# 16-bit denominators with queries split on GpSimd, a bias that ScalarE writes, and VectorE's sums of squares moved behind the split of qz

## The reference, cut to what matters

```python
def reference(x, ...):                      # x: 2 x 4096 x 512, float32
    x = x + _layernorm(_L0_attn_ref(_layernorm(x), w_qkv, w_proj, b_proj))
    x = x + _layernorm(_L0_ffn_ref(_layernorm(x), ...))

def _L0_attn_ref(x, w_qkv, w_proj, b_proj): # 16 heads of 32
    q, k, v = jnp.split(x @ w_qkv.T, 3, axis=-1)
    q, k = relu(q), relu(k)
    ksum = k.sum(over the sequence)
    z = 1.0 / (jnp.einsum('bhd,bhdn->bhn', ksum, q) + eps)
    context = jnp.einsum('bhdn,bhen->bhde', v, k)
    out = jnp.einsum('bhde,bhen->bhdn', context, q) * z
    return out @ w_proj.T + b_proj
```

## Time and profile before

| | us |
|---|---|
| median of 3 runs | 2459.85 (2457.72 to 2460.81) |
| the profiled execution | 2460.71 |
| its span, first to last instruction | 2458.9 |

### The profile page before, as it was taken

How to read it: one execution, slowest core, us unless ns; L and a number is a source line. 1 busy time by engine, 2 the same in 40 slices (tenths; PEclk the granted TensorE clock), 3 DMA queues, 4 the chain that set the end, 5 groups by cost and what they waited for, 6 DMA issues and landing times.

```text
span 2458.9 us, 56923 instructions
## 1 busy us (share of the span) xinstructions
PE 2400.0 (98%) x20208; PEld 1433.9 (58%) x20208; DVE 1805.9 (73%) x3548; ACT 1580.2 (64%) x3473; POOL 1136.8 (46%) x929
## 2 busy tenths in 40 slices
PE   5999999998999999999999999999999999999997
PEld 2444444454666666666666666666666666666664
DVE  5444444426888888888888888888888888888885
ACT  3222323226777777777777777777777777777774
POOL 2587533313444444444444444444444444444444
PEclk9999999999999999999999999999999999999999
DMA  5634434311111111111111111111111111111111
GB/s 137 202 99 126 103 103 102 85 56 35 40 47 47 51 43 47 43 43 43 43 44 50 50 45 48 43 43 43 43 43 47 50 48 46 43 43 43 43 29 32
DMA packets 250704, 145.65 MB, mean 59 GB/s; under 512 B 208096, under 2 KB 208096, under 8 KB 250144
## 3 DMA queue, kind: packets, MB, share of 16 engines
q1 hardware_dynamic: 240048, 119.32, 19.6%
q10 hardware_dynamic: 9504, 17.31, 1.9%
q0 software_dynamic: 1104, 8.40, 0.9%
HBM read 61.09 MB, written 33.55 MB: 38 GB/s over the span
## 4 chain that ended last, share of the span: by engine, by line
PE 93%; POOL 3%; DVE 2%; ACT 1%; issue 1%; DMA 1%; POOLq 0%; SPq 0%; DVEq 0%; ACTq 0%
PE psum L319 17%; PE psum L320 16%; PE psum L321 16%; PE psum L592 6%; PE psum L457 5%; PE psum L494 5%; PE psum L447 4%; PE psum L474 4%; PE psum L503 3%; PE psum L514 2%; PE psum L331 2%; PE psum L368 2%; PE psum L367 2%; PE psum L466 2%; PE psum L366 1%; PE psum L429 1%
## 5 line engine op out<-in xcount | busy, mean ns | idle before, releaser
L319 PE MATMUL psum<-wb,region 128*128 128x512 f16 x768 | 293.0, 381 | 0.0
L320 PE MATMUL psum<-wb,region 128*128 128x512 f16 x768 | 291.6, 380 | 0.0
L321 PE MATMUL psum<-wb,region 128*128 128x512 f16 x768 | 291.6, 380 | 0.0
L1077 POOL TENSOR_TENSOR region<-region,kfac 128x512 f32<-128x512 f32 x64 | 66.7, 1042 | 482.9 <-DVE kfac L1335 482.9
L1060 POOL TENSOR_TENSOR region<-region 128x1024 f32<-128x1024 f32 x64 | 147.8, 2309 | 258.7 <-DVE region L1443 230.2
L1443 DVE SCALAR_TENSOR_TENSOR region<-psum,region 128x512 f16<-128x512 f32 x64 | 44.2, 691 | 222.4 <-ACT region L887 222.4
L1065 POOL TENSOR_TENSOR region<-region 128x1024 f32<-128x1024 f32 x64 | 150.5, 2352 | 93.2 <-DVE region L1208 93.2
L1072 POOL TENSOR_SCALAR region<-region,m 128x512 f32<-128x512 f32 x256 | 172.3, 692 | 26.5 <-DVE hm L1279 26.5
L592 PE MATMUL psum<-region 128*128 128x512 f16 x768 | 176.2, 379 | 2.1 <-DVE region L1443 2.1
L1081 POOL TENSOR_TENSOR region<-region 128x512 f32<-128x512 f32 x64 | 81.8, 1277 | 202.7 <-ACT region L795 202.7
L1242 DVE SCALAR_TENSOR_TENSOR region<-psum,m,region 128x512 f32<-128x512 f32 x192 | 144.1, 751 | 6.8
(11 more groups left out here) (236 smaller groups left out, 7208.3 us busy)
## 6 DMA issues: line engine op xcount, KB each, us to landing
region<-x_in SPq DMA_DIRECT2D x128, 256.0 KB, 2.6
q_cols<-region ACTq DMA_DIRECT2D x64, 256.0 KB, 2.5
region<-q_cols SPq DMA_DIRECT2D x64, 256.0 KB, 2.8
out_rows<-region SPq DMA_DIRECT2D x62, 256.0 KB, 2.0
region<-wb_in POOLq DMA_DIRECT2D x1, 3072.0 KB, 13.4
region<-wqkv_in SPq DMA_DIRECT2D x4, 512.0 KB, 6.9
region<-region SPq DMA_TRANSPOSE x128, 3.0
region<-ws_in POOLq DMA_DIRECT2D x1, 1280.0 KB, 7.6
```

What stands on the lines that cost most here:

```text
L319: mm(out, lhs(0), rhs(0), start=start, stop=False)
L320: mm(out, lhs(0), rhs(1), start=False, stop=False)
L321: return mm(out, lhs(1), rhs(0), start=False, stop=stop)
```

## The change

The denominators are made of 16-bit parts: the sums of the keys are scaled, split (`ks16`) and put into two block matrices (`kden`), and GpSimd splits the loaded queries of tile n+3 in step n (`ahead_queries`), between `front_k2` and `front_state`; `den` waits for that (`q16_ok`) and issues 12 products in place of 4. The bias is no product any more: ScalarE copies it to the bank (`ahead_bias`), after it has waited for VectorE's qz, and the products add to it. VectorE's `back_norm` stands behind `ahead_qz_split`. The queries are stored with their scale of 64, and the factors of the totals are changed to suit; GpSimd no longer prepares `bias16`. The transposed copies of ScalarE signal once per path in place of twice.

```diff
--- before.py
+++ after.py
@@ -80,9 +80,9 @@
...
-        bias16 = sb("bias16", C, dt=f16)
...
-        kden = sb("kden", BATCH, KT, P)
+        kden, ks16 = sb("kden", 2, BATCH, KT, P, dt=f16), sb("ks16", 2, BATCH * KT, dt=f16)
+        q16 = sb("q16", 2, 2, KT, P, dt=f16)
...
@@ -321,21 +321,26 @@
...
             def den(n, p, b, at=0, back=True):
-                pe.wait_ge(S(f"qb{p}_in"), loads(n, p))
+                pe.wait_ge(S("q16_ok"), n * 2 + 2)
...
-                    last = mm(bank[at][:, g * P:(g + 1) * P], kden[:, b, g, :], qb[:, p, g, :], start=True, stop=True)
+                    to = bank[at][:, g * P:(g + 1) * P]
+                    mm(to, kden[:, 0, b, g, :], q16[:, p, 0, g, :], start=(g == 0), stop=False, skip_group_check=True)
+                    mm(to, kden[:, 0, b, g, :], q16[:, p, 1, g, :], start=False, stop=False, skip_group_check=True)
+                    last = mm(to, kden[:, 1, b, g, :], q16[:, p, 0, g, :], start=False, stop=True, skip_group_check=True)
...
             def y_mm(n, b, at=0):
...
-                mm(bank[at], ones16[:, :], bias16[:, :], start=True, stop=False)
+                pe.wait_ge(S("bias_ok"), n + 1)
...
-                    last = mm3(bank[at], lambda x: qz16[:, x, g, :], lambda x: mix[b][:, x, g, :], False, g == KT - 1)
+                    mm(bank[at], qz16[:, 0, g, :], mix[b][:, 0, g, :], start=False, stop=False, skip_group_check=True)
+                    mm(bank[at], qz16[:, 0, g, :], mix[b][:, 1, g, :], start=False, stop=False, skip_group_check=True)
+                    last = mm(bank[at], qz16[:, 1, g, :], mix[b][:, 0, g, :], start=False, stop=(g == KT - 1), skip_group_check=True)
...
@@ -448,9 +453,8 @@
...
             def scores(n, path):
-                kT, qT, where, k_ready, q_ready = ((k1T, q1T, (2, 5), "k1T_ok", "q1T_ok"), (k2T, q2T, (4, 6), "k2T_ok", "q2T_ok"))[path]
-                pe.wait_ge(S(q_ready), cur(n))
-                pe.wait_ge(S(k_ready), cur(n))
+                kT, qT, where, ready = ((k1T, q1T, (2, 5), "path1_ok"), (k2T, q2T, (4, 6), "path2_ok"))[path]
+                pe.wait_ge(S(ready), cur(n))
@@ -687,9 +691,9 @@
...
-            def to_cols(n, dst, where, k, done):
+            def to_cols(n, dst, where, k):
...
-                ac(dst.rearrange("p a b -> p (a b)"), bank[where], ACT.Copy).then_inc(S(done), 1)
+                return ac(dst.rearrange("p a b -> p (a b)"), bank[where], ACT.Copy)
...
@@ -726,6 +730,10 @@
...
+            def ahead_bias(n, at=0):
+                act.wait_ge(S("qzf_ok"), n + 1)
+                ac(bank[at], bproj[:, :], ACT.Copy, scale=QZ_SCALE).then_inc(S("bias_ok"), 1)
...
@@ -803,12 +811,12 @@
             def front_transposed(n):
...
-                to_cols(n, q1T, 5, 0, "q1T_ok")
-                to_cols(n, k1T, 2, 1, "k1T_ok")
+                to_cols(n, q1T, 5, 0)
+                to_cols(n, k1T, 2, 1).then_inc(S("path1_ok"), 1)
...
             def front_transposed2(n):
-                to_cols(n, q2T, 4, 2, "q2T_ok")
-                to_cols(n, k2T, 6, 3, "k2T_ok")
+                to_cols(n, q2T, 4, 2)
+                to_cols(n, k2T, 6, 3).then_inc(S("path2_ok"), 1)
...
@@ -852,6 +860,7 @@
...
+                    ahead_bias(n + 2)
@@ -890,8 +899,7 @@
...
-                ac(q4[:, :, m, :], bank[3].rearrange("p (t c) -> p t c", t=GT), ACT.Relu,
-                   scale=1.0 / W_SCALE).then_inc(S("q_read"), 1)
+                ac(q4[:, :, m, :], bank[3].rearrange("p (t c) -> p t c", t=GT), ACT.Relu).then_inc(S("q_read"), 1)
...
@@ -948,7 +956,9 @@
...
+            ahead_bias(0)
...
+            ahead_bias(1, at=5)
@@ -1012,9 +1022,6 @@
             def late_bias():
...
-                then_step(nc.gpsimd.tensor_scalar(bias16[:, :], bproj[:, :], 1.0, 1.0, ALU.mult, ALU.mult))
-                low = slice(HALF, P)
-                then_step(nc.gpsimd.tensor_tensor(bias16[low, :], bproj[low, :], bias16[low, :], ALU.subtract))
...
@@ -1104,12 +1111,23 @@
...
-            def step(n, p, front=True, back=True):
+            def ahead_queries(n, p, again=True):
+                wait_alone(pool, S(f"qb{p}_in"), loads(n, p))
+                if again:
+                    wait_alone(pool, S("den_pe"), n)
+                nc.gpsimd.tensor_scalar(q16[:, p, 0], qb[:, p], 1.0, 1.0, ALU.mult, ALU.mult).then_inc(S("q16_ok"), 1)
+                pool.wait_ge(S("q16_ok"), n * 2 + 1)
+                nc.gpsimd.tensor_tensor(q16[:, p, 1], qb[:, p], q16[:, p, 0], ALU.subtract).then_inc(S("q16_ok"), 1)
...
+            def step(n, p, front=True, back=True, ahead=True):
...
+                if ahead:
+                    ahead_queries(n + 3, 1 - p)
+                if front:
@@ -1137,13 +1155,18 @@
...
+            ahead_queries(0, 0, again=False)
+            ahead_queries(1, 1, again=False)
...
+            ahead_queries(2, 0)
...
-            with pool.Fori(1, ALL - 1, 2) as n:
+            with pool.Fori(1, ALL - 3, 2) as n:
...
-            step(ALL - 1, 1)
-            step(ALL, 0, front=False)
+            step(ALL - 3, 1, ahead=False)
+            step(ALL - 2, 0, ahead=False)
+            step(ALL - 1, 1, ahead=False)
+            step(ALL, 0, front=False, ahead=False)
@@ -1400,9 +1423,6 @@
...
-                if back:
-                    back_norm(m)
-                if front:
@@ -1411,6 +1431,8 @@
...
+                if back:
+                    back_norm(m)
@@ -1464,15 +1486,22 @@
...
+                totals = flat(ksum_c[:, :, :])
+                ve.tensor_scalar(ks16[:, 0], totals, W_SCALE / SEQ, None, ALU.mult).then_inc(S("ctx_ok"), 1)
+                dve.wait_ge(S("ctx_ok"), 2)
+                ve.scalar_tensor_tensor(ks16[:, 1], totals, W_SCALE / SEQ, ks16[:, 0], ALU.mult, ALU.subtract).then_inc(S("ctx_ok"), 1)
+                dve.wait_ge(S("ctx_ok"), 3)
...
-                ve.tensor_scalar(flat(ksum_q[:, :, :]), flat(ksum_c[:, :, :]), TINY, QZ_SCALE, ALU.max, ALU.mult).then_inc(S("ctx_ok"), 1)
+                ve.tensor_scalar(flat(ksum_q[:, :, :]), flat(ksum_c[:, :, :]), TINY, QZ_SCALE / W_SCALE, ALU.max, ALU.mult).then_inc(S("ctx_ok"), 1)
...
-                dve.wait_ge(S("ctx_ok"), 4)
+                dve.wait_ge(S("ctx_ok"), 6)
...
             def key_blocks(b):
-                ve.tensor_tensor(kden[:, b, :, :], blocks.unsqueeze(1).to_broadcast([P, KT, P]), wide(ksum_c[:, b, :], P),
-                                 ALU.mult).then_inc(S("ctx_ok"), 1)
+                for x in range(2):
+                    last = ve.tensor_tensor(kden[:, x, b, :, :], blocks.unsqueeze(1).to_broadcast([P, KT, P]),
+                                            wide(ks16[:, x, b * KT:(b + 1) * KT], P), ALU.mult)
+                last.then_inc(S("ctx_ok"), 1)
```

More of the change, by code:

```diff
@@ L191, in sandwich_kernel @@
                        "low1_ok", "labi_ok", "lexp_ok", "abs_ok", "ex_ok", "ln_ok", "sig_ok",
-                       "v_ok", "ke_ok", "e1_ok", "e2_ok", "exs_ok", "q1T_ok", "k1T_ok", "q2T_ok", "k2T_ok",
+                       "v_ok", "ke_ok", "e1_ok", "e2_ok", "exs_ok", "path1_ok", "path2_ok",
                        "osq_ok", "z_ok", "ogh_ok", "xc_ok", "xnh_ok", "x1m_ok"],
@@ L481, in inter_sparse @@
                 pe.wait_ge(S("state_ok"), cur(n))
-                pe.wait_ge(S("q2T_ok"), cur(n))
+                pe.wait_ge(S("path2_ok"), cur(n))
                 pe.wait_ge(S("am1_ok"), cur(n))
@@ L620, in mixing @@
             def mixing(b):
-                pe.wait_ge(S("ctx_ok"), (6, 8)[b])
+                pe.wait_ge(S("ctx_ok"), (8, 10)[b])
                 pe.wait_ge(S("wproj_ok"), 1)
@@ L928, in mixed @@
             def mixed(b):
-                act.wait_ge(S("ctx_ok"), (6, 8)[b])
+                act.wait_ge(S("ctx_ok"), (8, 10)[b])
                 for g in range(KT):
```

## The result

The kernel after takes 2427.64 us (median of 4 runs, 2425.90 to 2429.88), the kernel before 2460.22 beside it on the same chip (2457.72 to 2460.81): a ratio of 0.9872, with an interval of 0.9861 to 0.9884. The direction held and so did most of the mechanism: the two products' worth came off TensorE's list as worked out. The sum left out a wait that went away and a gain in stage one. The profiled executions took 2460.71 and 2425.90 us, with spans of 2458.9 and 2424.1.

A forecast was written before the change was run, and what follows sets the result against it. TensorE's list of products was taken to bound stage two. 0.221 + 0.216 = 0.437 us a step over 62 steps made 27.1 us off 2460.7, 2433.6, less 0.9 for the median: 2433 us, range 2430.5 to 2437 (82 in 100).

The forecast's parts named there:

- 12 products of 0.0557 us: TensorE's denominators in 16 bits: 0.67 us against 0.89, a gain of 0.22 us a step.
- 0.21 by the bias: TensorE's list before the y products: one bias product fewer, worth 0.21 us a step.
- the order of waits on ScalarE, GpSimd and VectorE: Stage two: ScalarE waits for VectorE's qz, GpSimd's idle before the states goes, VectorE's carry waits for GpSimd's state.
- The rival on the pace of weight loads: TensorE's denominators: 81 ns a product gives 2452 us (3 in 100); 98 ns gives 2464, no change (2 in 100).
- ScalarE was not held up: Rival, 9 in 100: the moved sum brings qz no earlier, ScalarE's bias copy ends 0.5 us late; 2438 to 2445 us.
- GpSimd's two ops: Query split on GpSimd between k2 and the states: 0.62 and 1.16 us plus 0.1 wait, 1.87 us a step.
- the baseline of a step: Stage two: one whole step takes 29.13 us, with TensorE busy in all of it.
- 0.13 too late: Before TensorE's y products: without the moved sum of squares, qz would stand 0.13 us late, the move's worth.
- stage one at nothing: Once-only work: GpSimd loses two small ops in stage one; no gain was counted for it.
- GpSimd's tolerance: GpSimd between k2 and the states: slacks 1.23 + 0.26 + 0.58 + 0.51 give 2.58 us before TensorE stands.
- the last rival: Slower, 4 in 100: GpSimd's ops past 2.58 us delay VectorE's carry and the gates product; 2505 us if they take double.
- the start's 2 us: Steps 0 and 1: TensorE's wait for qz may shift the start by about 2 us either way.

The follow-up runs named there:

- the repeated execution: The kernel after run once more, unaltered, against the kernel before: 2427.11 us, ratio 0.9874.
- the last version: Kernel after with queries' split ahead of k2, centring of output weights spread over two tiles, bias prepared at tile 33: 2426.69 us, 0.9869 of the kernel before.

## Why the prediction was right, and where it failed

**Right.** TensorE's list sets the end; 12 products of 0.0557 us; 0.22 saved by them and 0.21 by the bias; a step of 28.69, as the prediction has it word for word (the 59 average 28.693); the order of waits on ScalarE, GpSimd and VectorE. The rival on the pace of weight loads fell with the 0.67 us of the denominators. By the 81 ns of the Trainium skill (TensorE: Matmul & The Clock Gate, section Back-to-back issue gap) the 12 would have taken 0.97; the trace, with 0.67, does not agree with it here. ScalarE was not held up: it has no idle behind the copy, and TensorE none before the y products. GpSimd's two ops took 1.87 us, start of the first to end of the second, exactly the term; another 0.1 went by before the states began (1507.07 to 1507.18).

**Failed: the baseline of a step.** The prediction took 29.13 us, one whole step, for all, with TensorE waiting for nothing in it, and its sum is 62 x 0.437 and no term for a wait that goes away. But every second step took 29.21, because the y products waited 0.08 us for qz. It read the margin wrongly: "Without the move, qz would stand at 1521.75, 0.13 too late: that is what the move is worth." The move is worth 2.26 us with nothing else changed, and 0.25 a step (14.68 in 59) with the rest in place, since without it the denominators' 0.22 are lost too (2.26 + 12.97 would be 15.23). The 0.13 is too small by the 0.07 us from the end of the split to the first y product, which makes 0.20, and by the 0.08 of every second step. Both parts share one wait: 2.26 for the move, 12.97 for the denominators behind it, 12.60 for the bias are the 27.83 measured. At 0.437, 59 steps would be 25.8. The step in the earlier trace rows was one of the four around the change of the batch, outside VectorE's loops: no wait was to be seen in it, and only a series of steps showed the alternation.

**Failed: stage one at nothing.** "GpSimd loses two small ops in stage one" stands in the prediction among what comes out even, with no cover named. They had none; 1.69 us.

**Mis-sized, without effect here: GpSimd's tolerance.** "In all GpSimd can spend [...] 2.58 us before TensorE stands" adds four idles as if each were free. The carry came 0.58 late against the 0.4 forecast, and the next 1.24 us cost 0.875. The room was there for 1.87 us, but with some 0.37 us to spare, not 0.71. So the last rival (a slower kernel through GpSimd's state) was nearer than its price of 2.58 us said: one more op of 1.16 us, 1.24 with its gap, made it true.

**The sum.** 32.6 us between the medians: 27.8 from the 59 steps, 1.7 from stage one, about 1.3 from the steps at either end (1.2 at the start; 0.1 at the end, if the repeated execution's 91.53 is taken in place of 89.66). The remaining 1.8 I put to what varies from one execution to the next: the interval of the ratio is 28.5 to 34.2 us, and the other comparisons with the same step gave 31.3 for the repetition, 33.5 and 30.5 for the two versions with the split moved and 31.1 for the last version, with the five at 31.8 on average. In which stretch the 1.8 lie, if anywhere, can't be settled by these runs. The forecast's 27.1 was 25.8 for the 59 steps and 1.3 for the others, so its shortfall of 5.5 is 2.0 (the alternation), 1.7 (stage one) and this 1.8. The range had taken "the start's 2 us" as the only unknown outside the steps, and no room for a term costed at nothing.

## What to carry to other kernels

Before a saving is counted, find the wait that comes next behind it on the same engine, and measure several consecutive steps inside the loop, not one beside it: a step length that alternates by 0.08 us betrays a near tie that no list of waits shows, and what lies ahead of the tie is worth nothing until the tie is moved. Slacks along a chain can be added only if the chain ends; where it comes back to its start within a step, as it seems to here, less is left than their sum (0.37 us here, not 0.71). And the place in the queue decides whether an op draws on it: the same op cost 51.6 us behind k2 and nothing ahead of it. An op that is taken away can save time too: look up what stands behind it (1.69 us here). And before a stretch is used as a measure, see how much it varies between executions of the same code.

## What was not expected of the hardware

VectorE's tiny decay op, 128x20 with two inputs in SBUF, took 0.17 us in the kernel before and 0.90 after: it starts at 1506.20 and ends at 1507.10, 0.03 after GpSimd's low part of the queries (1505.90 + 1.17 = 1507.07), and with the split elsewhere it takes 0.17 again (1505.00 above, where GpSimd is idle). From 1000 to 2000 us all 35 of these ops took 0.88 to 0.91 us in the kernel after, against 0.17 in both others; over some 60 steps that is about 45 of the 48 us that VectorE is busy longer. It looks like VectorE standing still for GpSimd's instruction. The Trainium skill (SBUF — State Buffer, section SBUF: two separate sides) states such an exclusive hold for the whole instruction, and the trace agrees; the prediction had weighed it only as VectorE blocking GpSimd, and here the small op was the one that waited. It cost TensorE nothing. GpSimd's states began 0.08 us after its end, as they did in the kernel before (1525.47 and 1525.55), and so about 0.1 us later than their own queue allowed; that came out of GpSimd's room.
